# Graph network kernel on one core: gates, norm, projections and graph run chunk by chunk in one phase, and two of the eight level sums move into the attention loop

## What is computed

```python
# layer 0: A = adj without its diagonal, d = its diagonal
ns = A @ x
for each head h in 0..2:                      # attention
    hW = x @ W[h]; hp = (A > 0) @ hW; e = leaky_relu(hp @ a1[h] + ...)     # one score per node
    att = softmax(where(A > 0, e[None, :], -9e15), axis=1)
    es += (att * A) @ hW / 3
edge = gru(ns, x, edge weights);  node = gru(es, x, node weights)
x1 = layernorm(x + d * (edge + node))
# gru(i, h): r, z = sigmoid(i @ Wi + h @ Wh + b); n = tanh(i @ Win + bi + r * (h @ Whn + bh)); (1 - z) * n + z * h
# layer 1 (no row has more than 350 entries, so top-k keeps all)
F = tanh(adj * adj) where adj > 0
g = tanh(x1 @ W_proj + b_proj) @ W_gcn
out = layernorm(x1 + relu(F @ g + b_gcn))
```

## Time and profile before

| | us |
|---|---|
| median of the runs (1446.6 to 1449.61) | 1446.94 |
| the profiled execution | 1447.55 |
| its span, first to last instruction | 1444.5 |
| TensorE busy | 1351.0 (94%) |
| VectorE busy | 1062.0 (74%) |
| ScalarE busy | 909.6 (63%) |

### The profile page before, as it was taken

The page is one execution under the profiler, slowest core; times in us unless marked ns, Lnnn a source line. Parts: engine busy times, 40 slices in busy tenths (PEclk is TensorE's granted clock), DMA queues, the critical chain, the costliest instruction groups (busy, mean ns, idle before and its releaser), DMA issues. The chain is left out here.

```text
span 1444.5 us, 11276 instructions
## 1 busy us (share of the span) xinstructions
PE 1351.0 (94%) x3652; PEld 616.4 (43%) x3652; DVE 1062.0 (74%) x1312; ACT 909.6 (63%) x952; POOL 46.2 (3%) x68
## 2 busy tenths in 40 slices
PE   5999999798799999999999999999979967999996
PEld 4444444255344444444444444444434433444442
DVE  1344333446799999999999999999828868475773
ACT  2655455313598788888878888888625546465553
POOL 0000000100010010010100100100000000000000
PEclk9999999989899999999999999999989978999998
DMA  7878888213224233332333424231062108878822
GB/s 261 333 275 275 286 275 288 60 35 158 103 87 151 98 116 131 102 146 88 125 123 105 143 88 160 88 108 66 1 243 83 44 4 320 317 294 299 300 98 60
DMA packets 53823, 228.80 MB, mean 158 GB/s; under 512 B 9928, under 2 KB 15752, under 8 KB 36232
## 3 DMA queue, kind: packets, MB, share of 16 engines
q1 hardware_dynamic: 51200, 225.55, 44.0%
q10 hardware_dynamic: 2568, 2.58, 0.5%
HBM read 223.82 MB, written 4.29 MB: 158 GB/s over the span
## 5 line engine op out<-in xcount | busy, mean ns | idle before, releaser
L1115 PE MATMUL t_y_ps<-mask,x_sb 128*128 128x512 f32 x1536 | 666.2, 596 | 15.2 <-DVE mask L1045 15.2
L1115 PEld LDWEIGHTS t_y_ps<-mask,x_sb 128*128 128x128 f32 x1536 | 293.1, 191 | 385.0 <-issue 368.1
L1045 DVE TENSOR_TENSOR mask<-mask 128x1536 f32<-128x1536 f32 x256 | 450.0, 1759 | 2.1 <-ACT mask L893 2.1
L893 ACT ACTIVATE mask<-mask,ones 128x1536 f32<-128x1536 f32 x256 | 399.3, 1560 | 1.1 <-DVE mask L1031 1.1
L886 ACT ACTIVATE mask<-mask,t_minus_e 128x512 f32<-128x512 f32 x256 | 184.6, 721 | 89.9 <-PE t_y_ps L1115 88.2
L1031 DVE TENSOR_SCALAR mask<-mask,e_cols 128x512 f32<-128x512 f32 x512 | 228.5, 488 | 13.7 <-PE t_y_ps L1115 9.9
L282 PE MATMUL ns_ps<-pieces,x_sb 128*128 128x512 f32 x512 | 229.0, 603 | 7.0 <-POOL pieces L150 7.0
L1682 PE MATMUL p_ff_ps<-mask,p_g_all 128*128 128x512 f32 x512 | 223.8, 598 | 9.1 <-ACT mask L1621 9.1
L1682 PEld LDWEIGHTS p_ff_ps<-mask,p_g_all 128*128 128x128 f32 x512 | 97.6, 192 | 129.5 <-issue 120.3
L282 PEld LDWEIGHTS ns_ps<-pieces,x_sb 128*128 128x128 f32 x512 | 96.7, 193 | 129.6 <-issue 129.4
L167 ACT ACTIVATE signs<-pieces 128x2048 fp8e4<-128x2048 f32 x64 | 122.3, 1911 | 46.7 <-DMA pieces<-in_adj_c 25.3
(11 more groups left out here) (178 smaller groups left out, 629.8 us busy)
## 6 DMA issues: line engine op xcount, KB each, us to landing
pieces<-in_adj_c SPq DMA_DIRECT2D x64, 1024.0 KB, 5.0
mask<-in_adj_c SPq DMA_DIRECT2D x64, 1024.0 KB, 4.8
mask<-in_adj_t SPq DMA_DIRECT2D x32, 2048.0 KB, 8.7
mask<-scratch_shifts SPq DMA_DIRECT2D x8, 1536.0 KB, 8.1
pieces<-in_x_t SPq DMA_DIRECT2D x1, 2048.0 KB, 11.5
scratch_ns_t<-ns_sb ACTq DMA_DIRECT2D x8, 256.0 KB, 5.9
p_g_x_t<-in_x_t SPq DMA_DIRECT2D x8, 256.0 KB, 2.9
p_g_ns_t<-scratch_ns_t SPq DMA_DIRECT2D x8, 256.0 KB, 3.1
```

The source lines that it names most:

```text
L893: nc.scalar.activation(t, t, ACT.Exp, bias=ones[:, :], scale=-1.0).then_inc(exped, 1)
L1045: nc.vector.tensor_tensor(term(n), term(n), a, ALU.mult).then_inc(terms, 1)
L1115: mm = nc.tensor.matmul(y_ps[c % 2][h][:, :], x_sb[:, k, :], term(n)[:, h, :], start=k == 0, stop=k == NB - 1)
```

## The change

1. *Middle.* Only six level sums (`EARLY`) come ahead of the loop. VectorE does chains 0 to 3 and three gaps, then the loop, with chains 4, 5, 6, 7 after n = 1, 4, 10, 15. TensorE does level sums 6 and 7 after n = 5 and 10. ScalarE's and TensorE's small steps are spread accordingly. The weights of the tail are loaded at the start of this phase.
2. *Tail.* `tail_phase` takes the place of the gate, norm and graph phase. Iteration c makes the gates and cells of chunk c and everything up to g of chunk c - 1. Both cells share four PSUM banks; one bank (`mid_ps`) serves all transposes and projections; three hold the sums of graph chunks 0 to 2. The graph is 64 units of 1 MB (chunk, group of four tiles), read from `adj_c`, the layout of the attention, in a ring of eight. A group of the first three chunks needs g of one chunk only: three units go with each iteration, 21 in all before the last g. The other units follow. The inverse root is made on VectorE, per chunk of rows, from an integer seed and three Newton steps, in place of Sqrt and reciprocal; for the outputs it is made chunk by chunk too.

The diff, cut to its core:

```diff
 # middle_phase, sync
             load_small(nc, sp, dram, keep)
+            load_tail_weights(sp, dram, keep)      # 8 loads, first waited for in the tail
 # scalar
-            for c in range(NCHUNK - 1):
+            for c in range(EARLY - 1):
                 take_out(c)
...
-            among = {0: lambda: shift_exps_of(last - 1), 1: lambda: (take_out(last), rows_out(last - 2)), 3: lambda: rows_out(last - 1),
-                     4: lambda: shift_exps_of(last), 10: lambda: rows_out(last)}
+            among = {2: lambda: (take_out(5), shift_exps_of(4)), 3: lambda: rows_out(3), 6: lambda: shift_exps_of(5), 7: lambda: rows_out(4),
+                     10: lambda: take_out(6), 12: lambda: shift_exps_of(6), 13: lambda: rows_out(5), 15: lambda: take_out(7),
+                     17: lambda: shift_exps_of(7), 20: lambda: rows_out(6), 25: lambda: rows_out(7)}
 # vector
-            for c in range(NCHUNK - 2):
+            for c in range(EARLY - 2):
                 chain(c)
             for n in range(AHEAD):
                 gap(n)
-            chain(NCHUNK - 2)
+            chains = {1: 4, 4: 5, 10: 6, 15: 7}
             for n in range(NB * NCHUNK):
...
-                if n == 1:
-                    chain(NCHUNK - 1)
+                if n in chains:
+                    chain(chains[n])
 # tensor
-            for c in range(NCHUNK):
+            def level_sums(c):
...
+            for c in range(EARLY):
+                level_sums(c)
-            among = {0: lambda: turn_sums(last), 1: lambda: turn_shifts(last - 1), 8: lambda: turn_shifts(last)}
+            among = {2: lambda: turn_sums(5), 3: lambda: turn_shifts(4), 5: lambda: level_sums(6), 7: lambda: (turn_sums(6), turn_shifts(5)),
+                     10: lambda: level_sums(7), 12: lambda: turn_sums(7), 15: lambda: turn_shifts(6), 20: lambda: turn_shifts(7)}
 # tail_phase
+LOCK, G_RING, NEWTON = 3, 8, 3
+    first = [[(c, g) for c in range(LOCK)] for g in range(NPIECE)]
+    rest = [(c, g) for c in range(LOCK, NCHUNK) for g in range(NPIECE)]
+    units = [u for group in first[:-1] for u in group] + rest[:4] + first[-1] + rest[4:]
+ # sync
+            load_in(0); load_in(1)                          # x_t and ns_t of a chunk
+            for u, (c, g) in enumerate(units):
+                if u >= G_RING:
+                    sp.wait_ge(products, u - G_RING + 1)
+                sp.dma_start(piece(u)...)
+                if u < (NCHUNK - 2) * LOCK and u % LOCK == LOCK - 1:
+                    load_in(u // LOCK + 2)                  # waits cells, u // LOCK + 1
+ # scalar, for c in range(NCHUNK + 1); what has c - 1 only if c, what has c only if c < NCHUNK
+                read_gates("edge", c); make_n("edge", c)
+                square_rows(c - 1, ...); tanh(3 * (c - 1))
+                read_gates("node", c); tanh(3 * (c - 1) + 1); make_n("node", c)
+                make_h2(c - 1); tanh(3 * (c - 1) + 2); copy_g(c - 1)
+            for u in range(24, 64):
+                tanh(u)                                     # relu(c) at u == done_at[c] + 1
+                                                            # square_rows(c, y2) at u == done_at[c] + 5
+ # vector
+                pre_n("edge", c)                            # waits for the three reads
+                make_y(c - 1); center(c - 1, ...); square_a(3 * (c - 1)); make_cell("edge", c)
+                finish_x(c - 1)                             # inverse_root, then scaling
+                pre_n("node", c); square_a(3 * (c - 1) + 1); copy_x(c - 1)
+                make_cell("node", c); add_cells(c); square_a(3 * (c - 1) + 2)
+            for u in range(24, 64):
+                square_a(u)                                 # add_x1(c) at u == done_at[c] + 4
+                                                            # finish_y2(c) at u == done_at[c] + 7
+ # tensor; gates(k, c) waits until the other cell's gates are read and its pre_n is done
+                gates("edge", c); turn_cells(c - 1)         # waits copied >= c - 1: g of chunk c - 2
+                graph(3 * (c - 2)); gates("node", c); turn_x(c - 1)
+                graph(3 * (c - 2) + 1); project(c - 1); graph(3 * (c - 2) + 2); features(c - 1)
+            for u in range(21, 64):
+                graph(u)                                    # turn_features(c) at u == done_at[c] + 2
+ # inverse_root(c): t = s / H + eps, v = -t / 2, seed, three times (r * r, * v, (+ 1.5) * r), each step waiting for the last
+                nc.vector.tensor_scalar(out.bitcast(I32), t.bitcast(I32), -0.5, ROOT_SEED, ALU.mult, ALU.add).then_inc(step, 1)
```

More of the change, by code:

```diff
@@ L730 @@
 ON_DVE = 2
+EARLY = 6
 SHIFT_AT = (0, 22528)
@@ L903, in _ @@
             act.wait_ge(negated, 1)
-            last = NCHUNK - 1
-            among = {0: lambda: shift_exps_of(last - 1), 1: lambda: (take_out(last), rows_out(last - 2)), 3: lambda: rows_out(last - 1),
-                     4: lambda: shift_exps_of(last), 10: lambda: rows_out(last)}
+            among = {2: lambda: (take_out(5), shift_exps_of(4)), 3: lambda: rows_out(3), 6: lambda: shift_exps_of(5), 7: lambda: rows_out(4),
+                     10: lambda: take_out(6), 12: lambda: shift_exps_of(6), 13: lambda: rows_out(5), 15: lambda: take_out(7),
+                     17: lambda: shift_exps_of(7), 20: lambda: rows_out(6), 25: lambda: rows_out(7)}
             gap(0)
@@ L1095, in _ @@
                                           mask[:, c, k, :], start=k == 0, stop=k == NB - 1)
-                    if k == 7 and c:
+                    if k == 7 and 0 < c < EARLY:
                         turn_sums(c - 1)
-                    if k == 24 and c >= 2:
+                    if k == 24 and 2 <= c < EARLY:
                         turn_shifts(c - 2)
                 mm.then_inc(sums_done, 1)
+            for c in range(EARLY):
+                level_sums(c)
             last = NCHUNK - 1
-            among = {0: lambda: turn_sums(last), 1: lambda: turn_shifts(last - 1), 8: lambda: turn_shifts(last)}
+            among = {2: lambda: turn_sums(5), 3: lambda: turn_shifts(4), 5: lambda: level_sums(6), 7: lambda: (turn_sums(6), turn_shifts(5)),
+                     10: lambda: level_sums(7), 12: lambda: turn_sums(7), 15: lambda: turn_shifts(6), 20: lambda: turn_shifts(7)}
             pe.wait_ge(w_ready, 16)
@@ L1498, in _, with graph_units, load_tail_weights @@
                 mm.then_inc(multiplied, 1)
+LOCK = 3
+G_RING = 8
+G_AT = G_RING * PW
+Y2_AT = G_AT + N
+X1T_AT = Y2_AT + N
+H2T_AT = X1T_AT + 2 * CW
+FT_AT = H2T_AT + 2 * CW
+NEWTON = 3
+ROOT_STEPS = 3 + 3 * NEWTON
+ROOT_SEED = 1597463007.0
+def graph_units():
+    first = [[(c, g) for c in range(LOCK)] for g in range(NPIECE)]
+    rest = [(c, g) for c in range(LOCK, NCHUNK) for g in range(NPIECE)]
+    return [u for group in first[:-1] for u in group] + rest[:4] + first[-1] + rest[4:]
+def load_tail_weights(engine, dram, keep):
+    for k in KINDS:
+        engine.dma_start(keep["wih"][k][:, :], dram[k + "_Wih_t"]).then_inc(keep["w_loaded"], 16)
+        engine.dma_start(keep["whh"][k][:, :], dram[k + "_Whh_t"]).then_inc(keep["w_loaded"], 16)
+    engine.dma_start(keep["w_proj"][:, :], dram["W_proj"]).then_inc(keep["w_loaded"], 16)
+    engine.dma_start(keep["w_gcn"][:, :], dram["W_gcn"]).then_inc(keep["w_loaded"], 16)
+    engine.dma_start(keep["b_proj"][:, :], dram["b_proj"].unsqueeze(1)).then_inc(keep["w_loaded"], 16)
+    engine.dma_start(keep["b_gcn"][:, :], dram["b_gcn"].unsqueeze(1)).then_inc(keep["w_loaded"], 16)
@@ L1534, in graph_phase @@
         m = Mem(nc, ctx, keep["tag"])
-        a_t = [keep["first_a_t"] if prefetched else m.sb(tag + "f_t0", [P, CHUNK, N]),
-               keep["second_a_t"] if "second_a_t" in keep else m.sb(tag + "f_t1", [P, CHUNK, N])]
+        a_t = [keep["first_a_t"] if prefetched else m.sb(tag + "f_t0", [P, CHUNK, N]), m.sb(tag + "f_t1", [P, CHUNK, N])]
         b_gcn = m.sb(tag + "b_gcn", [P, 1])
@@ L1814, in build @@
                     flat = keep["mask"][:, :, :, :].rearrange("p c k n -> p (c k n)").bitcast(F32)
-                    halves = flat.rearrange("p (b r n) -> p b r n", b=2, r=CHUNK)
                     keep["flat"], keep["es"] = flat, flat[:, ES_AT:ES_AT + N]
-                    keep["first_a_t"], keep["second_a_t"] = halves[:, 0, :, :], halves[:, 1, :, :]
+                    ml = Mem(nc, last, keep["tag"])
+                    keep["wih"], keep["whh"] = ({k: ml.sb(k + w, [P, 3 * H]) for k in KINDS} for w in ("_wih", "_whh"))
+                    keep["w_proj"], keep["w_gcn"] = ml.sb("w_proj", [P, H]), ml.sb("w_gcn", [P, H])
+                    keep["b_proj"], keep["b_gcn"], keep["w_loaded"] = ml.sb("b_proj", [P, 1]), ml.sb("b_gcn", [P, 1]), sem("h_w_loaded")
                     middle_phase(nc, sem, dram, keep)
[L1819 to L1822, removed]
+                    tail_phase(nc, sem, dram, keep)
                 ahead.close()
-        spare.extend(sems[name] for name in sorted(sems) if name.startswith(("l_", "q_")))
```

(2 more changed lines are left out.)

321 lines of the change are left out of this document (added).

## The result

The changed kernel takes 1462.12 us (median of four runs, 1460.84 to 1463.92), the kernel before, on the same chip, 1448.28 (1446.6 to 1452.01). The ratio is 1.009, 95% interval 1.0072 to 1.0108: slower by 13.8 us. The forecast was 1465.6, slower, range 1449 to 1478. The profiled execution took 1461.51 us with a span of 1459.6, against 1447.55 and 1444.5.

What follows compares the result with a forecast made beforehand. TensorE's work was taken to bound attention and graph phase, leaving gains only in the hole ahead of attention and the 146.7 us between. Terms -4.5 + 7.0 + 7.5 + 7 + 1.65 = +18.65 gave 1465.6 us, range 1449 to 1478.

Steps and rivals of the forecast that it cites:

- rival (1): Whole kernel: slower as forecast, by the summed terms, 1465.6 us; chance 0.47.
- Middle, -4.5: New order of the level sums: attention products start earlier, but chains among terms starve TensorE; -4.5 us, bounds -6.5 and 0.
- Start of the tail: First gates wait for x and ns alone, weights being there already; first gate at 1063.0 us.
- Ring, +7.0: Tail's lock phase (gates, cells, three graph units per iteration): VectorE and ScalarE form a ring, 26.85 us a cycle; +7.0 us.
- Clock, +7.5: Lock phase: TensorE's recurring waits drop its clock in half the cycles, plus first and last; +7.5 us, bounds 0 and 12.
- Behind the lock phase, +7: Chunks 0 to 2 end together, VectorE's work holds TensorE up before unit 38; +7 us, bounds 2 and 11.
- Last root, +1.65: Last chunk's outputs: twelve small steps take 2.3 us where variance, root and reciprocal took 0.65; +1.65 us.
- (2): Lock phase: the ring isn't the bound, its handoffs hide behind TensorE's 23.2 us of work; faster, 1436.5 us; chance 0.1.
- It does not set the pace: Lock phase: TensorE's own work per cycle, 54 passes or 23.2 us, is not what bounds the cycle.
- (3): Tail: the clock holds and the hump at units 30 to 38 is half (3.5 us); 1454.6 us; chance 0.22.
- (4): Middle gains nothing, since chains queued among terms starve TensorE longer than laid out; 1470 us; chance 0.11.
- (5): Tail: the clock drops at every wait, in the hump too (12 and 11 us); 1474 us; chance 0.1.

Runs made afterwards that it cites:

- e4: Changed kernel with, on TensorE, the second graph unit ahead of the turn of x and the third ahead of the projection: 1458.18 us.
- e3: Changed kernel with, on ScalarE, the n of the node cell ahead of the tanh of the second graph piece: 1460.36 us.
- e7: Changed kernel with the ends of the chunks spread over the graph units by a table, so chunks 0 to 2 no longer end together: 1456.07 us.
- e12: e10 with, on ScalarE, the tanh of the projection ahead of the tanh of the second graph piece: 1416.78 us.
- e1: Kernel before with the new order of the level sums (middle) alone; gate, norm and graph phase as before: 1445.03 us.
- e10: e9 with the third graph unit in halves around the projection, and VectorE's copy of the turned x ahead of the second square: 1430.27 us.
- e2: Changed kernel with the old order of the level sums, so the new tail alone: 1465.41 us.
- e9: Changed kernel with the edits of e3, e4, e7 and e8, and the third graph piece's tanh behind the next chunk's edge n on ScalarE: 1425.12 us.
- e8: Changed kernel with TensorE's level sums 6 and 7 behind tiles 1 and 4 in place of 5 and 10: 1453.23 us.

## Why the prediction came out as it did

It went as rival (1), the forecast, 3.5 us over the median of the result. Term by term, on the profiled executions:

- **Middle, -4.5.** From chain 3's reciprocal to the copy of the last scores: 334.06 to 1058.15 before = 724.1, 719.7 after: -4.4. The layout by hand held in kind (waits behind chains 4 and 5, of 4.87 and 2.81 us, slow passes behind both). Tile 16 starts at 411.75, and chain 3 was 1.0 late: between the 408.9 without and the 412.2 with slow passes. What I did not ask was whether the level sums, whose work I had counted, could stand in these waits.
- **Start of the tail.** First gate at 1059.96, 4.3 after SP's first issue (1055.66): foretold 4 (3.6 in the sum).
- **Ring, +7.0.** Chunk 0's edge pre_n comes 8.0 us behind the first gate (foretold 7.9), chunk 1's 21.7 (21.3). The first cycle that carries no slow units is 26.58, and so is e4's with the clock at full speed: 26.85 was 1% over. The waits named (node n 2 us, reads 4) are there with 1.99 and 4.9. TensorE's wait for x is 2.13, not 4: the node gates, which follow a unit of 3.6 us, end 9.1 behind pre_n (1143.63 + 1.02 - 1135.53), not 7.3.
- **Clock, +7.5: the term that was mis-sized.** The clock did drop in each of five cycles, not in half of them, but a drop cost 1.7 us of slow passes (5.29 for 3.60), not up to 2.7. Of these 1.4 lengthen TensorE's loop (27.28 less the 25.89 in e3), and it had 0.7 to spare against the ring (the sum said 0.9): 0.7 us reach the cycle (27.28 less 26.58), 3.5 in all. The 1 in the first cycle and the 2 in the last did not show: features of chunk 7 end 227.3 behind the first gate, against 225.2 + 7.5, so the ring and this term together were 5.4 too large, 4.0 of it here (3.5 for 7.5) and 1.4 in the ring. The Trainium skill (TensorE: Matmul & The Clock Gate, HAM oscillation) has the low clock back after each wait that recurs between bursts. The trace of the kernel after agrees for six cycles in a row, with 5.29 us for the unit behind each wait for the scaled x; exceptions are its last such wait (2.79 us at 1278.15, then 3.60 for the unit) and the one of e3 at 1121.45. By my pricing of that rule the term would have been 12.
- **Behind the lock phase, +7.** From there to the last relu 157.7 (1287.3 to 1444.92), 0.2 of it behind the last product, where 150.0 had been the floor: +7.5. The five waits for tanh are at units 33 to 37, 5.3 us; e7 shows their cause. The size came out near, but 150.0 is not quite the floor: in e7, without the five waits, the same stretch takes 150.9 (1286.84 to 1437.8).
- **Last root, +1.65.** The steps take 0.20 each; relu to the end of the span is 1459.6 - 1444.92 = 14.7, before 13.06: +1.6.

Sum: -4.4 + 0.3 (last scores to first gate 5.16, foretold 4.85) + 16.5 (last relu 384.96 behind the first gate, against 368.4) + 1.6 = 14.0, and with 1.0 of late start 15.0 of the 15.1 between the spans. The prediction's terms add up to 18.65, so they were 4.65 too large: 5.4 in the ring and the clock, less 0.8 that the start of the tail and the stage behind the lock phase took more. The late start, which no term had, hides 1.0 of this: that part of the closeness is luck. One sentence of the prediction doesn't carry what it says: 8 cycles of 27 plus 150 are 366, and so are 8 of 12 plus 45 plus 225; the loss of the tail rested on its longer sum, 375.2 against 368.2.

**The rivals.** (2), the ring is not the bound, is refuted: e4 gives the ring at 26.58. But a cycle of the kind that it described came once the queue order was mended (e12's 23.23). The ring held as a mechanism; what it lacked is that a second loop of nearly its length runs beside it. TensorE's way round, from the scaled x to the next reads, was the longer by 0.7 in each cycle with a slow unit (ScalarE waits 0.58 for z in each of them) and the shorter by 0.7 at full clock, so the prediction's sentence "It does not set the pace" was right for TensorE's work and wrong for its loop as it ran; its paragraph on the clock had priced that, and nothing in it said that mending one loop alone would gain almost nothing. (3) fell with the clock at 0.94 and the whole hump there. (4) is refuted by e1, (5) by the clock of 1.00 behind the lock phase and by the 3.5 us that the drops cost in it.

## What to carry to other kernels

When two chains close over the same handoffs, each queue move alone looks nearly worthless (1.8 and 3.9 us here, 17.7 together): list every loop with its length, and change the order of all that are within a few per cent of the longest. Work without a deadline, here the graph's tanh, square and units, belongs behind every step that another engine waits for and inside the waits that remain, and it has to be placed on each of the engines it crosses: e10 moved a square on one and lost on the next. Here a pipeline that only takes phase borders away lost 15.6 us as a ring of waits (27.28 a cycle) and won 12 once its order was mended (24.27 a cycle), near the 23.2 of the busiest engine's own work.

## What the runs showed of the hardware

- **A short wait drops the clock in some executions and not in others.** The same wait of 2.05 us ahead of the same six passes at the end of the attention was followed by 4.54 us of them in the kernel before, 4.54 in e2, 4.38 in e7, 4.25 after, 4.14 in e9, 4.10 in e8, and by 2.84, full speed, in the other eight. In e3 the first wait of 2.14 us for the scaled x was followed by a unit at full speed (3.60), with the clock at 1.00 from 1120 to 1147; from 1147 to 1174 it was 0.94.
- **Where a wait of 2.1 us recurs each 27 us, the low clock is there in each cycle** of the kernel after (0.94 over the window, 5.29 for 3.60) and in all but that one of e3; only the last wait for the scaled x (2.79 us at 1278.15 in the kernel after) is followed by a unit of 3.60. Where it is 0.25 us (e4, whose other waits in the cycle are 0.7 to 1.4) or absent (e12), the clock stays at 1.00.
- **Up to 5 us of a run are settled in the support phase**, which all kernels share: TensorE's first score product starts at 277.06 in the kernel before, 277.83 after, 281.37 in e3, 281.71 in e8 and 281.82 in e1. What decides it I did not trace. A single profiled execution can't tell 3 us; measured from a point behind it, it can.
